# A graph layer's block loop: ids loaded a block ahead, h stored in five pieces, later gathers, an ending by halves

## What is computed

```
h      = relu(layernorm(x))
m      = h[src] + edge_attr                    # one row for each edge
aggr   = segment_sum(m, dst, 6250)             # one row for each node
hidden = relu(aggr @ W1 + b1)                  # 96 -> 192
out    = x + (1 + eps) * h + hidden @ W2 + b2
```

## Time and profile before

| | us |
|---|---|
| runs | 523.12, 524.78, 526.30; median 524.78 |
| the profiled execution | 525.66 |
| its span, from the first to the last instruction | 523.8 |
| PE busy / PEld busy | 471.7 / 449.8 |
| DVE busy / ACT busy / POOL busy | 483.0 / 414.5 / 298.1 |
| mean granted clock of TensorE | 0.984 of full speed |
| DMA | 110.03 MB, 210 GB/s over the span |

### The profile page before, as it was taken

The page is one execution under the profiler, slowest core; times in us unless marked ns, Lnnn a source line. Parts: engine busy times, 40 slices in busy tenths (PEclk is TensorE's granted clock), DMA queues, the critical chain, the costliest instruction groups (busy, mean ns, idle before and its releaser), DMA issues.

```text
span 523.8 us, 22553 instructions
## 1 busy us (share of the span) xinstructions
PE 471.7 (90%) x9174; PEld 449.8 (86%) x9174; DVE 483.0 (92%) x727; ACT 414.5 (79%) x637; POOL 298.1 (57%) x188
## 2 busy tenths in 40 slices
PE   0426999599999999999999999999999999999995
PEld 0315999499999899999999999999999999999994
DVE  8999999599999899999999998899999899999970
ACT  1798888488888777888888788888888888887871
POOL 1420000788888888688888888888888881000000
PEclk9997899899999999999999999999999999999998
DMA  8678987999889997999988799998888896775000
GB/s 239 221 217 261 273 226 203 257 240 219 229 223 239 279 220 194 256 255 266 224 217 222 179 206 273 250 266 211 232 199 190 212 239 163 205 210 150 6 10 21
DMA packets 96901, 110.03 MB, mean 210 GB/s; under 512 B 68934, under 2 KB 70586, under 8 KB 96664
## 3 DMA queue, kind: packets, MB, share of 16 engines
q1 hardware_dynamic: 74888, 98.39, 63.9%
q0 software_dynamic: 21904, 10.13, 15.5%
HBM read 102.00 MB, written 6.48 MB: 207 GB/s over the span
## 4 chain that ended last, share of the span: by engine, by line
PE 79%; DVE 9%; ACT 5%; issue 4%; DMA 1%; SPq 1%; DVEq 0%; ACTq 0%
PE agg_ps L1089 31%; PE oct_ps L1077 22%; PE agg_ps L1083 14%; PE key_ps L1101 5%; PE mlp_ps L1106 4%; DVE lo_hot L599 2%; ACT adj L921 2%; ACT gathered_edges L957 2%; DVE hot L606 2%; DVE z L599 1%; PE key_ps L1094 1%; DMA dst<-in_dst 1%; DMA gathered_edges<-in_dst 1%; ACT hid L934 1%; DVE agg L796 0%
## 5 line engine op out<-in xcount | busy, mean ns | idle before, releaser
L921 ACT ACTIVATE adj<-oct_ps 128x784 f16<-128x784 f32 x360 | 299.8, 865 | 74.6 <-PE oct_ps L1077 69.9
L528 POOL DMA_INDIRECT gathered_edges<-h_rows,gather_src x144 | 262.3, 1822 | 48.7 <-issue 41.2
L1089 PE MATMUL agg_ps<-hl,adj 128*128 128x192 f16 x2205 | 233.8, 246 | 0.2 <-ACT adj L921 0.2
L599 DVE TENSOR_TENSOR lo_hot<-iota_z,key 128x2048 f16<-128x2048 f16 x180 | 218.9, 1216 | 0.0
L1077 PE MATMUL oct_ps<-z,lo_hot 128*128 128x98 f16 x2880 | 191.7, 209 | 12.3 <-DVE lo_hot L599 6.6
L1077 PEld LDWEIGHTS oct_ps<-z,lo_hot 128*128 128x128 f16 x2880 | 165.6, 99 | 14.9 <-issue 8.2
L1089 PEld LDWEIGHTS agg_ps<-hl,adj 128*128 128x128 f16 x2205 | 174.1, 98 | 2.8 <-ACT adj L921 0.5
L599 DVE TENSOR_TENSOR z<-z_marks,key 128x1568 f16<-128x1568 f16 x180 | 174.0, 966 | 0.0
L1083 PE MATMUL agg_ps<-edges,hot 128*32 128x96 f32 x3240 | 78.5, 252 | 2.3 <-DVE hot L752 2.3
L1083 PEld LDWEIGHTS agg_ps<-edges,hot 128*32 128x32 f32 x3240 | 69.1, 112 | 7.8 <-DVE hot L752 2.6
L490 POOL DMA_INDIRECT win<-packed_keys,row_i x23 | 27.7, 1206 | 70.7 <-DMA gathered_edges<-in_edge_attr 63.4
(11 more groups left out here) (145 smaller groups left out, 193.5 us busy)
## 6 DMA issues: line engine op xcount, KB each, us to landing
edges<-in_edge_attr SPq DMA_DIRECT2D x180, 432.0 KB
gathered_edges<-in_edge_attr SPq DMA_DIRECT2D x16, 432.0 KB
dst<-in_dst SPq DMA_DIRECT2D x180, 4.5 KB
gathered_edges<-h_rows,gather_src POOLq DMA_INDIRECT x144
out<-ob SPq DMA_DIRECT2D x45, 48.0 KB
packed_keys<-adj SPq DMA_DIRECT2D x1, 1632.0 KB, 5.9
h_rows<-gathered_edges SPq DMA_DIRECT2D x1, 1200.0 KB, 13.2
h_rows<-gathered_edges SPq DMA_DIRECT2D x1, 1152.0 KB, 8.9
```

Of the source, the lines that this page charges most:

```text
L528: nc.gpsimd.indirect_dma_start(out=gathered[k][:, g, t, :], out_offset=None, in_=h_dram, in_offset=bass.IndirectOffsetOnAxis(ap=gather_src ...
L599: return nc.vector.tensor_tensor(out.rearrange("p t (w two) -> p t w two", two=2), marks[0:out.shape[0], 0:width].rearrange("p (o w two) - ...
L921: return nc.scalar.activation(adj[k][:, :, 2 * OCT * o:2 * OCT * (o + 1)].rearrange("p h (t q) -> p t h q", q=2), oct_ps[:, o % 2, :].rear ...
L1089: last = nc.tensor.matmul(agg_ps[buf][:, 0:2 * C], adj[buf][:, h, :], hl[:, h, :], start=False, stop=(h == NT - 1), skip_group_check=True)
```

## The change

- **Loads.** `load` becomes `load_ids` and `load_edges`, each with a value_load of its own for each group. Before the loop SP loads ids and edges of blocks 0 to 2 and the ids of block 3. In its turn of block b it loads the ids of block b + 1 (after waiting for the one-hots of block b - 2), then waits for the edge buffer, then loads the edges of block b.
- **h.** Its home is now gather buffer two and 13 rows behind it; it overlaps buffer one no more. It is stored in five pieces of ten rows (the last of nine), one in each turn of blocks 3 to 7. The residual is folded in 16 pieces (15 of three rows, one of four), one a block.
- **Gathers.** The buffer of attached block j is `j % 2`. The gather loads are in the turns of blocks 8, 16, 20 and 30; the first waits for no store of h. POOL fetches three key windows ahead of the gathers (one before), then waits for all pieces of h, and paces the gathers from block 6 on (block 4 before). The attached blocks follow main blocks 16, 26, 34 and 42.
- **The end.** All of block 44's slots are summed ahead of project of block 43; hidden, relu and project of block 44 go by halves, in two PSUM banks.

```diff
-ATTACHED = (14, 24, 34, 42)
-TAIL_CUTS = (8, 18, 34)
+ATTACHED = (16, 26, 34, 42)
+TAIL_CUTS = (8, 18)
-ROWS_FROM = 4
+ROWS_FROM = 6
-RES_FIRST = 36
-RES_ROWS = 6
+H_ROWS = 10
+RES_ROWS = 3
...
-        gather_home = sb("gathered_edges", [P, 2, GROUPS, GT, C])
+        gather_home = sb("gathered_edges", [P, GATHER_ROWS + NT, C])
-        h_sb = gather_home[:, :, :, :, :].rearrange("p k g t c -> p (k g t c)")[:, 0:NT * C].rearrange("p (t c) -> p t c", c=C)
+        h_sb = gather_home[:, GATHER_ROWS:GATHER_ROWS + NT, :]
...
-        RES = [(RES_FIRST, NT)] + [(t, t + RES_ROWS) for t in range(0, RES_FIRST, RES_ROWS)]
+        RES_SHARED = GATHER_ROWS // RES_ROWS
+        RES = [(t, t + RES_ROWS) for t in range(0, GATHER_ROWS, RES_ROWS)] + [(NM, NT)] + [(t, min(t + RES_ROWS, NM)) for t in range(GATHER_ROWS, NM, RES_ROWS)]
...
-            return (j + 1) % 2
+            return j % 2
+        def last_hidden(j):
+            return key_ps[0:C, TURN_AT:TURN_AT + P] if j == 0 else oct_ps[0:C, 0, 0:P]
...
-            def load(b):
+            def load_ids(b):
                 k = b % TURN
                 for g in range(GROUPS):
                     e0 = sp.value_load(...)
                     sp.dma_start(dst_sb[k][:, g, :], ...).then_inc(ids_in[k], 16)
+
+            def load_edges(b):
+                k = b % TURN
+                for g in range(GROUPS):
+                    e0 = sp.value_load(...)
                     sp.dma_start(edge_rows(b)[:, g, :, :], ...).then_inc(edges_in[k], 16)
+            def store_h(piece):
+                t0, t1 = H_ROWS * piece, min(H_ROWS * (piece + 1), NT)
+                sp.wait_ge(h_ready, 1 if t1 <= HALF else 2)
+                sp.dma_start(h_dram[t0 * P:t1 * P, :]..., h_sb[:, t0:t1, :]).then_inc(h_stored, 16)
...
-            load(0)
-            load(1)
-            load(2)
+            for b in range(TURN):
+                load_ids(b)
+                load_edges(b)
             sp.wait_ge(tab_ready, SPLITS)
+            sp.wait_ge(gather_hot, 1)
+            load_ids(TURN)
             for b in range(TURN, NM):
+                if b + 1 < NM:
+                    sp.wait_ge(narrow_ready, b - TURN + 1)
+                    load_ids(b + 1)
                 sp.wait_ge(edges_done, b - TURN + 1)
-                load(b)
-                if b == TURN:
-                    ...
-                if b == TURN + 2:
-                    sp.wait_ge(h_stored, 32)
-                    sp.wait_ge(res_ready, 1)
+                load_edges(b)
+                if TURN <= b < TURN + H_PIECES:
+                    store_h(b - TURN)
+                if b == TURN + 5:
+                    sp.wait_ge(words_ready, 1)
+                    sp.wait_ge(steps_ready, 1)
                     load_gathered(0)
-                if b == TURN + 2 + len(RES):
-                    sp.wait_ge(res_ready, len(RES))
+                if b == TURN + 1 + RES_SHARED:
+                    sp.wait_ge(h_stored, 16 * H_PIECES)
+                    sp.wait_ge(res_ready, RES_SHARED)
                     load_gathered(1)
...
-            fetched = WINS + 1
-            fetch(WINS)
-            pool.wait_ge(h_stored, 32)
+            fetched = WINS + 3
+            for q in range(WINS, fetched):
+                fetch(q)
+            pool.wait_ge(h_stored, 16 * H_PIECES)
...
-                        if ((j * GROUPS + g) * GT + t) * FETCH_PER >= (fetched - WINS - 1) * FETCH_EVERY and fetched < MPAIRS:
+                        if ((j * GROUPS + g) * GT + t) * FETCH_PER >= (fetched - WINS - 2) * FETCH_EVERY and fetched < MPAIRS:
...
+            next_join(NM - 1)
             finish(NM - 2)
-            next_join(NM - 1)
             finish(NM - 1)
...
-            for n in range(NM - 2, NM):
-                next_turned(n)
-                next_relu(n)
+            next_turned(NM - 2)
+            next_relu(NM - 2)
+            next_turned(NM - 1)
+            act.wait_ge(out_done, NM - 1)
+            for j in range(H):
+                act.wait_ge(last_hid_done, j + 1)
+                nc.scalar.activation(hid[0:C, j, :], last_hidden(j), ACT.Relu, bias=b1_sb[:, j:j + 1]).then_inc(last_hid_ready, 1)
...
-            sum_slots((NM - 1) % 2, TAIL_CUTS[1], TAIL_CUTS[2])
+            sum_slots((NM - 1) % 2, TAIL_CUTS[1], NT).then_inc(agg_done, 1)
             next_project(NM - 2)
-            sum_slots((NM - 1) % 2, TAIL_CUTS[2], NT).then_inc(agg_done, 1)
             next_turn(NM - 1)
-            next_hidden(NM - 1)
-            next_project(NM - 1)
+            pe.wait_ge(aggT_ready, NM)
+            for j in range(H):
+                nc.tensor.matmul(last_hidden(j), w1_sb[:, j, :], aggT[:, :], start=True, stop=True).then_inc(last_hid_done, 1)
+            output_free(NM - 1)
+            for j in range(H):
+                pe.wait_ge(last_hid_ready, j + 1)
+                last = nc.tensor.matmul(mlp_ps[:, OUT_AT:OUT_AT + C], hid[0:C + 1 - j, j, :], w2_sb[0:C + 1 - j, j, :], start=(j == 0), stop=(j == H - 1))
+            last.then_inc(out_done, 1)
```

More of the change, by code:

```diff
@@ L62, in build @@
     GE = P * GT
+    H_PIECES = -(-NT // H_ROWS)
+    GATHER_ROWS = GROUPS * GT
+    assert NT >= GATHER_ROWS and GATHER_ROWS % RES_ROWS == 0
     ELAST = E - GE
@@ L106, in build @@
         dst_sb = [sb(f"dst{k}", [P, GROUPS, GT], I32) for k in range(TURN)]
-        gather_home = sb("gathered_edges", [P, 2, GROUPS, GT, C])
-        gathered = [gather_home[:, k, :, :, :] for k in range(2)]
+        gather_home = sb("gathered_edges", [P, GATHER_ROWS + NT, C])
+        gathered = [gather_home[:, GATHER_ROWS * k:GATHER_ROWS * (k + 1), :].rearrange("p (g t) c -> p g t c", t=GT) for k in range(2)]
         gather_dst = [sb(f"gather_dst{k}", [P, GROUPS, GT], I32) for k in range(2)]
@@ L281, in build @@
         hid_ready = sem("hid_ready")
+        last_hid_done = sem("last_hid_done")
+        last_hid_ready = sem("last_hid_ready")
         out_done = sem("out_done")
@@ L326, in build @@
         THIRDS = [slice(0, 16), slice(16, 32), slice(32, NT)]
-        RES = [(RES_FIRST, NT)] + [(t, t + RES_ROWS) for t in range(0, RES_FIRST, RES_ROWS)]
+        RES_SHARED = GATHER_ROWS // RES_ROWS
+        RES = [(t, t + RES_ROWS) for t in range(0, GATHER_ROWS, RES_ROWS)] + [(NM, NT)] + [(t, min(t + RES_ROWS, NM)) for t in range(GATHER_ROWS, NM, RES_ROWS)]
+        assert 2 + RES_SHARED < ATTACHED[0] + 3
         def all_stored(engine):
@@ L377, in load @@
                     sp.dma_start(dst_sb[k][:, g, :], dst[bass.ds(e0, GE)].rearrange("(p t) -> p t", t=GT)).then_inc(ids_in[k], 16)
+            def load_edges(b):
+                k = b % TURN
+                for g in range(GROUPS):
+                    e0 = sp.value_load(e_tab[0:1, b * GROUPS + g:b * GROUPS + g + 1], min_val=0, max_val=ELAST)
                     sp.dma_start(edge_rows(b)[:, g, :, :], edge[bass.ds(e0, GE), :].rearrange("(p t) c -> p t c", t=GT)).then_inc(edges_in[k], 16)
@@ L387, in load_gathered @@
                     sp.dma_start(gather_dst[k][:, g, :], dst[bass.ds(e0, GE)].rearrange("(p t) -> p t", t=GT)).then_inc(gather_ids_in[k], 16)
+            def store_h(piece):
+                t0, t1 = H_ROWS * piece, min(H_ROWS * (piece + 1), NT)
+                sp.wait_ge(h_ready, 1 if t1 <= HALF else 2)
+                sp.dma_start(h_dram[t0 * P:t1 * P, :].rearrange("(t p) c -> p t c", p=P), h_sb[:, t0:t1, :]).then_inc(h_stored, 16)
             def store(b):
@@ L781, in finish @@
                 v.wait_ge(out_done, b + 1)
-                if b < RES_FIRST:
-                    v.wait_ge(res_ready, 2 + b // RES_ROWS)
+                v.wait_ge(res_ready, b // RES_ROWS + (1 if b < GATHER_ROWS else 2))
                 if b >= OBS:
@@ L805, in finish_gathered @@
                 v.wait_ge(gather_out_done, j + 1)
+                v.wait_ge(res_ready, RES_SHARED + 1)
                 if j >= 1:
```

## The result

The changed kernel takes **545.27 us** (median of 4 runs, 542.15 to 548.01) where the kernel before took 524.99 beside it: a ratio of 1.0382, 95% interval 1.0325 to 1.044. It is slower by 3.8%.

A forecast was written before the change was run, and what follows sets the result against it. The kernel before was taken as TensorE-bound with about 9 us of holes from SP, the changed one as SP-bound: 17.3 + 1.0 - 0.9 = 17.4 later, span 541.2, median 542 us, range 517 to 550.

The forecast's parts named there:

- The bound: Main loop: SP's added value_loads, 2.24 us a block, leave it no time to spare beside TensorE's 9.91.
- fast rival: Loop: SP's lateness stays inside the three edge buffers, the holes go, 9.7 us saved, 515 us; chance 0.22.
- SP's turn, 9.9: SP's work per loop block: 7.65 + 2.24 = 9.9 us, or 9.1 if no issue is stretched.
- I cost it at nothing: Stores of h in five pieces: three more issues, about 1.3 us, set against the 5.50 us hold that disappears.
- Block 31, 385.4: Edges of block 31 are there at 385.4 us, before 368.13: late by 17.3.
- the formula: Loop: edges of block b are there at 59.7 + 9.9 (b - 3) + 9.0 x (gather loads before) + 12.5.
- Block 17, 228.8: Edges of block 17 are there at 228.8 us, where the kernel before was at 226.48.
- a stall near SP's own: POOL's keys for block 10, fetched near 148 us: a stall near block 9's and about as long, 5 us.
- The rest takes as long as before: Behind block 31: no gather load is left and two attached blocks make TensorE slower than SP, so no further delay.
- Ids: VectorE's four waits for ids, 10.2 us in all, go; no wait for ids of comparable size was to show.
- SP at its least, POOL the last: Loop: SP's block is 9.1 us, POOL's late gathers and keys give back about 6 us, 521 us; chance 0.12.
- SP is in time: Loop: second value_load costs nothing or buffers absorb SP's lateness; holes and ending give 9.7 us, 515 us; chance 0.22.

The follow-up runs named there:

- room for POOL: Edit to three kernels: first three attached blocks two later, one more early key fetch, earlier fetches; on the changed kernel 540.33 us, with one table read 520.98.
- the kernel that looks ahead alone: Kernel before with only the ids loaded a block ahead, each group's table entry read once: 523.52 us, ratio 0.9964.

## Why the prediction was right, and where it wasn't

The forecast was 542 us for a slower kernel by SP, and it is that case: 545.27. Its steps, one by one:

- **The bound.** Shown by three pairs: the read added to the kernel before (+28.6), taken from the changed one (1.0382 to 1.0014), and taken away with POOL relieved (18 to 20 us on one chip). The Trainium skill (DMA: Bandwidth & Descriptors, Issuing engines are not separate DMA queues) calls the time to start one DMA usually small relative to the DMA. For one DMA the trace agrees: an id issue of 0.34 at 370.92, edges that landed 5.34 after their issue. The prediction's fast rival took this for a rule on the whole queue, which the section doesn't state; the sum of a turn's issues and register reads was 9.57.
- **SP's turn, 9.9.** Measured 9.57 in nine turns without a gather load, between the 9.1 and 9.9 of the text. The turns with a piece of h were longer: from 69.41 to 102.06 are three, 10.88 each. Here the step "I cost it at nothing" failed. SP is not held for 5.50 us any more, but each piece is an issue in a turn that has no room, and issues in these turns are stretched (one piece took 1.52 us, at 99.80). The five turns together, from 59.12 to 114.18, are 55.1 where 49.5 was forecast, 0.9 of it a wait for one-hots; that the pieces are what stretches them is not shown by a run of its own. TensorE waited for edges from blocks 7 and 8 on (1.48 and 1.05 us), and block 9's edges, forecast for 140.6, were used at 145.19.
- **Block 31, 385.4.** Measured 384.46. That it is this close is luck in part, because errors met. The first id issue, 59.7, was at 59.12. Of the 28 turns from there the five with a piece of h were 5.6 us too long together, the four with a gather load 0.3 (on average 9.4 more than 9.57, where 9.0 was forecast), and the other 19 were 7.3 too short together, at 9.52 each. So block 31's turn, 372.9 by the formula, began at 370.92. From there to the edges' use it was 13.5, not 12.5: the 4.2 to the landing was read from a row of ids, and edges took 5.34 here and 5.94 at 110.37.
- **Block 17, 228.8.** The formula is SP's, but TensorE came there at 238.61 for another reason: block 16 had waited 3.42 for its gathers and then ran at half clock. POOL was named for block 10 only, as "a stall near SP's own", its first gather, forecast near 130, came at 135.83, and the fetch, forecast near 148, at 151.89. That SP's delay hides POOL's in the end held: SP's turns run on without TensorE, so at block 31 SP was the last again, and room for POOL left the kernel with two reads at 540.33. In that kernel block 17 waits for edges and starts at 230.84, 2.0 behind the formula. At block 21, where the prediction also saw a wait, there was none in the changed kernel.
- **"The rest takes as long as before", plus 1.0 of clock, less 0.9.** This is the term that missed. From block 31 to the end is 546.1 - 384.46 = 161.6, before 523.8 - 368.13 = 155.7: 5.9 more where 0.1 was forecast. The half clock behind the stall cost 12.70 x 0.23 = 2.9, not 1.0. Another 3.3 lies at block 42, with the 1.90 of idle time ahead of 505.23 that the profile puts down to nothing, and a granted clock of 0.87 over the block; and 1.3 lies at block 34, with the 1.25 at 421.22. The cause of both stays open. The ending is 546.1 - 525.51 = 20.6 behind block 44's first sum, 1.4 less than the 22.0 before, by the row below from the chain of the kernel before: the upper end of the 0 to 1.4 that was forecast.

```profile
501.82 1.62 PE agg_ps L1083 x72
```

- **Ids.** The waits for ids were to go. One of 4.85 us remained, of a size that the prediction's signs had ruled out, for block 10, whose ids are behind the first gather load in SP's queue (137.78 above); block 9's edges were later still, so it decided nothing.
- **The rivals.** "SP at its least, POOL the last" was given 521. It is not what the change did, but what lies beneath it: with one read POOL's keys and gathers are what is late, at about 525. "SP is in time" was given 515; the kernels with one read and room for POOL came to 518.7 to 521. Its sum took every hole as a gain.

## What to carry to other kernels

Count what each queue issues per block, register reads too, and hold it against the block's time: a queue at 97% of the block wins back 0.3 us a turn of the 8.6 to 10.3 that it loses in one, and three buffers only put the stall off, here to block 7. When one loop over loads is split into two, keep the registers that both need. A wait that is removed by issuing something earlier can come back as a wait for what was pushed behind it, as at block 6 of the kernel that looks ahead alone. Spreading a long burst of issues over two turns took the waits for ids from 3.0 us to 0.7 here, without a gain in time that can be told from it.

## What the runs showed of the hardware

- A value_load, 0.56 us on SP, is more than half of the 1.03 of the two issues beside it. Four more of them for each block cost 18 to 20 us of 540, though SP had waited 62.8 us before.
- The half clock outlasts its stall: 3.30 us of idle time ahead of block 31 were followed by a block at 0.77, which cost 2.9 more.
- Edges issued on SP landed 5.34 us after the last issue at 378.99 began, 5.94 at 110.37, and 6.74 in the kernel that looks ahead alone, where four were issued in 2.73 us; the prediction's 4.2 is one row of ids.
